# Four cross-attention layers on one core: other orders of work at the layers' edges, and scores with the high and low parts of two heads in one stationary tile

## The chip, the core and the metric

The kernel runs on one NeuronCore of a Trainium2 chip. The metric is the device time of one launch in microseconds (us). The core has TensorE (PE; its weight loads are shown apart as PEld), VectorE (DVE), ScalarE (ACT), GpSimd (POOL), and SyncE (SP), which here issues the DMAs. Each engine runs its own instructions in order and meets the others at semaphores.

## The reference

Four cross-attention layers follow each other on a stream x of 8 batches of 512 tokens by 512 channels. The context has 77 rows of 1024 channels for each batch. Layers 0 and 2 have 16 heads of 64 channels, a bias on four context columns, and an output bias. Layers 1 and 3 normalise x first, and have 16 query heads of 32 channels on 4 key/value heads, so four query heads share the same keys.

```python
# layers 0 and 2
q = x @ Wq; k = ctx @ Wk; v = ctx @ Wv                # 16 heads of 64
logits = einsum('bhqd,bhkd->bhqk', q, k) * 64**-0.5 + col_bias
x = softmax(logits) @ v @ Wo + bo + x
# layers 1 and 3
xn = x * rsqrt(mean(x*x) + 1e-5) * norm_w
q = xn @ wq                                           # 16 heads of 32
k = ctx @ wk; v = ctx @ wv                            # 4 heads of 32
x = softmax(einsum('btgrd,bsgd->bgrts', q, k) * 32**-0.5) @ v @ wo + x
```

## The kernel before

**Numbers in two parts.** Every operand of a large matmul is held as a high part (an fp32r copy, made by ACT) and a low part (the rest, made by DVE or POOL). A product takes three passes into one PSUM bank: high by high, high by low, low by high (`three_passes`, L241 to L243).

**Stages.** A first stage (`context_part`, up to about 267 us) projects the context to keys and values of all layers and writes them to scratch memory. The main part (`whole_block`) runs 130 steps. A unit is one batch, one group of four heads, one layer: 32 units for each layer, kind A for layers 0 and 2 (units 0 to 31 and 64 to 95), kind B for layers 1 and 3 (units 32 to 63 and 96 to 127). In step s every engine works on several units at once: scores and softmax of unit s, queries of unit s+1, transposes of the probabilities of unit s-1 (`turn`, `turned(n)`), the product with the values of unit s-2 (`values`), and the output projection of a batch whose four units are done (`project`).

**Order.** The order is written out by hand for each engine, as a loop over s with one branch for kind A and one for kind B. In a B step TensorE does scores of token tiles 0 and 1, half of the next queries (6 matmuls), scores 2 and 3, a part of the values, `turned(0)`, the other half of the queries, the other values, `turned(1)`, at every fourth step the sums of squares (`stats`), `turned(2)` and the projections. ACT does the exponentials, then the high part of `turned(0)`, of the queries (`split_q`), of the values' product (`split_o`) and of `turned(1)` and `turned(2)`. DVE does for each of four tiles a maximum (L1110) and a subtraction (L1114) that frees the score bank, then a late projection result, the low part of `turned(0)` (L1137), the denominators (L1149, L1152), the low part of the queries (L1121), of the values' product (L1143) and of `turned(1)` (L1137) and `turned(2)` (L1134 in B, L1129 twice in A). There are two score banks, so scores of tile t wait until DVE has done tile t-2 (`s_sub`). In an A step ACT also writes a bias into the score bank ahead of the scores.

**Scores of kind B.** Four heads of 32 channels fill the 128 rows of the stationary tile (the queries). The moving tile is a block-diagonal 128 by 308: the keys of the group four times, 77 columns for each. Three passes of 308 columns make a token tile.

**Projections.** `Plan.projections(s)` says which of a batch's four output chunks are projected in step s: in layers 1 and 3 one chunk a step, at the end of layer 1 two a step; in layers 0 and 2 all four in one step, five steps after the batch began. For the last batch of layers 0 and 2 that is step 33 and step 97, which are B steps. `Plan.late(s)` names the chunk whose result DVE adds in the next step. The weights of a layer come in quarters (`PIECES`), each loaded by SP at the step after the one that consumed the quarter two before.

## Time and profile before

| what | value |
|---|---|
| median of 3 runs | 2091.65 us (2091.45 to 2092.06) |
| the profiled execution's own time | 2090.98 us |
| its span, first to last instruction | 2089.2 us |
| TensorE busy, share of the span | 2044.5 us, 98% |
| VectorE busy | 1390.2 us, 67% |
| ScalarE busy | 966.1 us, 46% |
| GpSimd busy | 644.7 us, 31% |

The table's last four rows are the first part of the profile's page. Busy time of TensorE counts the length of each matmul, and matmuls overlap, so the distance from one start to the next is what a matmul costs; the timeline gives it. The shares are means over stages with different limits.

### The profile page before, as it was taken

To read this page: it belongs to the slowest core of one execution; us is meant where nothing else is said; L and a number is where in the kernel's file an instruction comes from. 1 tells how busy PE (TensorE), PEld (TensorE's weight loads), DVE (VectorE), ACT (ScalarE), POOL (GpSimd) and SP (SyncE) were. 2 spreads that over 40 slices of the span, in tenths; PEclk is the share of its full clock that TensorE was granted. 3 is DMA by queue.
4 is the path that set the end of the run, shared out by engine and by line. 5 is a ranking of instruction groups with operands and counts; after the bars stand their busy time and mean duration, and the time that the engine had idled before them with its cause. 6 is when DMAs were issued, how large, how long until landed. Compare 5 with 4: busy or idle time off the path is not lost.

```text
span 2089.2 us, 31293 instructions
## 1 busy us (share of the span) xinstructions
PE 2044.5 (98%) x11546; PEld 1765.7 (85%) x11546; DVE 1390.2 (67%) x2408; ACT 966.1 (46%) x1814; POOL 644.7 (31%) x519
## 2 busy tenths in 40 slices
PE   8999999999999998999999999999999989999998
PEld 8999988888888886788888888888888867888886
DVE  5332365775568555888888676557755675888885
ACT  3222253553445344655554554335534553555552
POOL 1000042322232254454443341223222443444441
PEclk9999999999999999999999999999999999999999
DMA  7788832222122222343333332212221222333322
GB/s 214 168 171 200 190 91 63 72 67 73 53 72 70 65 75 68 92 108 93 93 90 94 104 96 64 77 53 71 66 73 52 73 85 67 80 91 86 85 72 82
DMA packets 262393, 191.02 MB, mean 91 GB/s; under 512 B 197506, under 2 KB 199970, under 8 KB 259682
## 3 DMA queue, kind: packets, MB, share of 16 engines
q1 hardware_dynamic: 262242, 189.03, 34.6%
q8 instruction: 92, 1.51, 0.3%
q14 instruction: 59, 0.48, 0.1%
HBM read 132.66 MB, written 56.26 MB: 90 GB/s over the span
## 4 chain that ended last, share of the span: by engine, by line
PE 90%; DVE 6%; ACT 1%; DMA 1%; issue 1%; SPq 1%; POOL 0%; DVEq 0%; ACTq 0%
PE acc_bank L846 11%; PE acc_bank L241 8%; PE acc_bank L243 8%; PE acc_bank L242 8%; PE q_bank L804 8%; PE q_bank L808 8%; PE q_bank L806 8%; PE t_bank L826 7%; PE ctx_bank L241 4%; PE ctx_bank L242 4%; PE ctx_bank L243 4%; PE s_bank L767 2%; PE s_bank L241 2%; PE s_bank L764 2%; PE s_bank L770 2%; PE s_bank L243 2%
## 5 line engine op out<-in xcount | busy, mean ns | idle before, releaser
L1262 POOL TENSOR_TENSOR prob<-prob,rinv 128x1232 f32<-128x1232 f32 x128 | 288.5, 2254 | 1044.1 <-DVE rinv L1152 1044.1
L1014 ACT ACTIVATE q_s<-q_bank 128x512 fp32r<-128x512 f32 x192 | 115.1, 599 | 532.9 <-PE q_bank L808 527.0
L846 PE MATMUL acc_bank<-pT_s,vals_s 128*128 128x512 f32 x1024 | 338.1, 415 | 0.0
L1110 DVE TENSOR_REDUCE mx<-s_bank 128x4 f32<-128x308 f32 x512 | 240.5, 470 | 125.7 <-PE s_bank L243 63.5
L804 PE MATMUL q_bank<-x_s,w_s 128*128 128x512 f32 x768 | 319.2, 416 | 4.0 <-POOL w_s L1255 4.0
L808 PE MATMUL q_bank<-x_s,w_s 128*128 128x512 f32 x768 | 313.9, 409 | 0.0
L806 PE MATMUL q_bank<-x_s,w_s 128*128 128x512 f32 x768 | 312.9, 407 | 0.0
L241 PE MATMUL acc_bank<-o_s,w_s 128*128 128x512 f32 x752 | 303.6, 404 | 2.5 <-DVE o_s L1143 2.5
L243 PE MATMUL acc_bank<-o_s,w_s 128*128 128x512 f32 x752 | 296.8, 395 | 0.0
L242 PE MATMUL acc_bank<-o_s,w_s 128*128 128x512 f32 x752 | 296.7, 395 | 0.0
L1005 ACT ACTIVATE prob<-prob,rstd 128x308 f32<-128x308 f32 x256 | 141.2, 555 | 287.3 <-DVE prob L1114 271.5
L1114 DVE TENSOR_TENSOR prob<-s_bank,mx 128x308 f32<-128x308 f32 x512 | 245.2, 479 | 27.4 <-DVE mx L1110 1.4
L1137 DVE TENSOR_TENSOR pT_s<-t_bank,pT_s 128x512 fp32r<-128x512 f32 x256 | 175.8, 687 | 82.3 <-ACT pT_s L1028 82.3
L1166 DVE SCALAR_TENSOR_TENSOR x_back<-acc_bank,bo,x_back 128x512 f32<-128x512 f32 x64 | 47.8, 747 | 259.5 <-PE acc_bank L243 259.5
L846 PEld LDWEIGHTS acc_bank<-pT_s,vals_s 128*128 128x128 f32 x1024 | 190.8, 189 | 28.5
L1028 ACT ACTIVATE pT_s<-t_bank 128x512 fp32r<-128x512 f32 (+1 forms) x320 | 183.3, 590 | 23.8 <-PE t_bank L826 23.6
L826 PE MATMUL t_bank<-ident,prob 128*128 128x128 f32 (+1 forms) x1280 | 184.5, 273 | 1.1 <-DVE pT_s L1137 1.1
L1149 DVE TENSOR_REDUCE sums<-prob 128x16 f32<-128x1232 f32 x128 | 182.5, 1426 | 1.9 <-ACT prob L997 1.9
L826 PEld LDWEIGHTS t_bank<-ident,prob 128*128 128x128 f32 (+1 forms) x1280 | 154.6, 136 | 28.2 <-DVE pT_s L1137 1.6
L241 PEld LDWEIGHTS acc_bank<-o_s,w_s 128*128 128x128 f32 x752 | 141.1, 188 | 34.9 <-DVE o_s L1143 4.1
L243 PEld LDWEIGHTS acc_bank<-o_s,w_s 128*128 128x128 f32 x752 | 141.0, 187 | 34.5
L242 PEld LDWEIGHTS acc_bank<-o_s,w_s 128*128 128x128 f32 x752 | 141.3, 188 | 30.8
(107 smaller groups left out, 4097.2 us busy)
## 6 DMA issues: line engine op xcount, KB each, us to landing
stream<-x_back SPq DMA_DIRECT2D x128, 256.0 KB, 2.6
x_front<-stream SPq DMA_DIRECT2D x96, 256.0 KB, 3.4
x_back<-stream SPq DMA_DIRECT2D x96, 256.0 KB, 4.0
kvw_raw<-kvw SPq DMA_DIRECT2D x17, 1024.0 KB, 8.4
k_scr<-k_out SPq DMA_DIRECT2D x36, 308.0 KB, 9.2
keys_s<-k_scr SPq DMA_DIRECT2D x128, 77.0 KB, 2.4
v_scr<-v_out SPq DMA_DIRECT2D x8, 1024.0 KB
vals_s<-v_scr SPq DMA_DIRECT2D x512, 6.5 KB
```

The source lines that it names most:

```text
L241: pe.matmul(out, weights[0], moving[0], start=start, stop=False)
L242: pe.matmul(out, weights[0], moving[1], start=False, stop=False)
L243: return pe.matmul(out, weights[1], moving[0], start=False, stop=stop)
L804: pe.matmul(out, w[0], x_now[0], start=k == 0, stop=False)
L806: pe.matmul(out, w[0], x_now[1], start=False, stop=False)
L808: mm = pe.matmul(out, w[1], x_now[0], start=False, stop=k == XC - 1)
L826: mm = pe.transpose(t_bank[(3 * u + n) % 2][0:rows, t * P:t * P + P], p, ident[:, :])
L846: mm = pe.matmul(out, w, pT_s[:, part], start=i == mine[0] and part == 2 * n and w is v[0], stop=i == mine[-1] and w is terms[-1][0] and p ...
L1028: act.activation(pT_s[0:rows, 2 * n], t_bank[(3 * u + n) % 2][0:rows, :], ACT.Copy).then_inc(t_hi, 1)
L1110: dve.tensor_reduce(top, scored, AX_X, ALU.max).then_inc(s_max, 1)
L1114: dve.tensor_tensor(prob[:, slot, t].rearrange("q (h n) -> q h n", h=GH), scored, top.unsqueeze(2).broadcast_to([P, GH, CTX]), ALU.subtrac ...
L1262: pool.tensor_tensor(view, view, rinv[:, slot].unsqueeze(2).broadcast_to([P, TILES * GH, CTX]), ALU.mult).then_inc(p_norm, 1)
```

## The change

It has five parts.

1. **Scores of kind B.** A stationary tile now holds 64 rows of high parts of two heads and 64 rows of low parts of the same two heads (`q_s[:, slot, 1, pair]`). The moving tile holds the high part of the keys in its first 154 columns, in every row block. Two matmuls of 154 columns give high by high and low by high for two heads each, and one of 308 columns gives high by low for all four. The keys' DMAs write the same bytes to other columns.
2. **Its operands.** For a B unit ACT makes three copies where it made one (128 rows, then 64 rows twice), and DVE two subtractions of 64 rows where it made one of 128. Each of DVE's two reads 64 rows of the bank and writes the other 64 rows of the tile.
3. **Last batch of layers 0 and 2.** Its four chunks are split between steps 33 and 34 (97 and 98). In step 34 (98), called `ahead`, they come before the values on TensorE, and DVE does the denominators and both results before `turned(0)`.
4. **Steps 0, 1, 31, 63 and 95** (`early`; it acts in the A branch alone). ACT and DVE do the split of the next queries later: the first after the bias of tile 2 (ACT) and after tile 1 (DVE), the second after `turned(1)`. In steps 0 and 1 TensorE spreads the queries over all four tiles.
5. **Weights.** In A steps SP loads the next quarters at the end of the same step instead of at the start of the next.

```diff
@@ Plan
+            projections = [("proj", gb, m) for gb, m in self.projections(s)]
+            if self.ahead(s):
+                acc += projections
             if 0 <= s - 2 < NU:
                 acc += [("pv", s - 2, m) for m in range(kind(s - 2).Q)]
-            acc += [("proj", gb, m) for gb, m in self.projections(s)]
+            if not self.ahead(s):
+                acc += projections
...
-        return found[-1:] if s < NU and kind(s).name == "B" else []
+        return found[-1:] if s < NU and kind(s).name == "B" and not self.ahead(s) else []
+    def ahead(self, s):
+        return 2 * GROUPS <= s < NU and s % (2 * UNITS) == UNITS + 2
+    def early(self, s):
+        return s < 2 or s + 1 < NU and kind(s + 1) is not kind(s)
...
                 elif layer == 1:
                     at += m // 2
+                elif layer % 2 == 0 and b == B - 1:
+                    at += m // 2
@@ sync
-                    keys = keys_s[:, slot].bitcast(F32).rearrange("q (h n) -> q h n", h=2)
                     for r in range(GH):
-                        sp.dma_start(keys[32 * r:32 * r + 32, :, CTX * r:CTX * r + CTX],
+                        keys = keys_s[32 * r:32 * r + 32, slot, 0:2 * CTX * (2 + r - r % 2)].bitcast(F32)
+                        sp.dma_start(keys.rearrange("q (h a n) -> q h a n", h=2, n=CTX)[:, :, r % 2],
                                      k1_scr[p, b, 32 * g:32 * g + 32]).then_inc(keys_loaded[slot], 16)
...
-                for n in plan.pieces(s - 1):
-                    if n + 2 < len(PIECES):
-                        load_weights(n + 2)
+                if s and kind(s - 1).name == "B":
+                    for n in plan.pieces(s - 1):
+                        if n + 2 < len(PIECES):
+                            load_weights(n + 2)
...
                     load_vals(s)
+                if s < NU and kind(s).name == "A":
+                    for n in plan.pieces(s):
+                        if n + 2 < len(PIECES):
+                            load_weights(n + 2)
@@ tensor
-                    keys = keys_s[:, slot].rearrange("q (h n) -> q h n", h=2)
-                    three_passes(pe, out[:, 0:SC], [q_s[:, slot, h, 0, tok] for h in range(2)],
-                                 [keys[:, h] for h in range(2)], True, True).then_inc(s_mm, 1)
+                    for pair in range(2):
+                        pe.matmul(out[:, PAIR * pair:PAIR * (pair + 1)], q_s[:, slot, 1, pair, tok],
+                                  keys_s[:, slot, 0:PAIR], start=pair == 0, stop=False, skip_group_check=True)
+                    pe.matmul(out[:, 0:SC], q_s[:, slot, 0, 0, tok], keys_s[:, slot, PAIR:PAIR + SC], start=False,
+                              stop=True, skip_group_check=True).then_inc(s_mm, 1)
...
-                if a:
+                if a and s < 2:
+                    for t in range(TILES):
+                        beside(scores(s, t), q, 6)
+                        if t >= 2:
+                            turned(t - 2)
+                    turned(2)
+                elif a:
...
                     run(scores(s, 3), 1)
+                    if plan.ahead(s):
+                        for gb, m in plan.projections(s):
+                            project(gb, m)
                     run(v, 3)
@@ scalar
-                    act.activation(q_s[:, u % 2, 0, m], q_bank[item % 2][:, :], ACT.Copy).then_inc(q_hi, 1)
+                    high = act.activation(q_s[:, u % 2, 0, m], q_bank[item % 2][:, :], ACT.Copy)
+                    if kind(u).name == "B":
+                        for pair in range(2):
+                            rows = slice(64 * pair, 64 * pair + 64)
+                            high = act.activation(q_s[rows, u % 2, 1, pair], q_bank[item % 2][rows, :], ACT.Copy)
+                    high.then_inc(q_hi, 1)
...
-                    next(q, None)
+                    if not plan.early(s):
+                        next(q, None)
                     bias(s, 2)
...
                     bias(s + 1, 1)
+                    next(q, None)
                     exps(s, 1)
@@ vector
+                        for pair in range(2):
+                            rows, other = slice(64 * pair, 64 * pair + 64), slice(64 - 64 * pair, 128 - 64 * pair)
+                            low = dve.tensor_tensor(q_s[other, u % 2, 1, pair], q_bank[item % 2][rows, :],
+                                                    q_s[rows, u % 2, 0, m].bitcast(F32), ALU.subtract)
...
-                    next(q, None)
+                    if not plan.early(s):
+                        next(q, None)
                     tile_scores(s, 1)
...
                         rest_o(s - 2, pv - 1)
+                    next(q, None)
                     denominators(s)
...
+                    if plan.ahead(s):
+                        denominators(s)
+                        for gb, m in plan.projections(s):
+                            add_result(gb, m)
                     turned(0)
-                    if s < NU:
+                    if s < NU and not plan.ahead(s):
                         denominators(s)
```

## Rows read from the trace of the kernel before

**Rows 1.** The page: busy us (share of the span) and instructions of each engine.
```profile
PE 2044.5 (98%) x11546; PEld 1765.7 (85%) x11546; DVE 1390.2 (67%) x2408; ACT 966.1 (46%) x1814; POOL 644.7 (31%) x519
```
**Rows 2.** Table by stretch, steps 109 to 112: length, busy us (x), granted clock, DMA.
```profile
1861.10:1903.90 42.80, 42.80 (x233) 36.50 (x232) 35.77 (x66) 23.63 (x45) 18.62 (x12) 1.00 0.34 90
```
**Rows 3.** Waits in the same stretch: who waited for whom, us in total, times, longest.
```profile
DVE mx L1110 <- PE s_bank L243: 3.9, 8, 1.3
```
**Rows 4.** Timeline of PE, an A step: start, length, engine, line, out<-in.
```profile
500.18 0.23 PE L764 MATMUL s_bank<-keys_s,q_s 128*128 128x154 f32 x1
...
500.98 0.24 PE L764 MATMUL s_bank<-keys_s,q_s 128*128 128x154 f32 x1
```
**Rows 5.** Timeline of PE, two B steps of the steady part.
```profile
1871.62 0.30 PE L241 MATMUL s_bank<-keys_s,q_s 128*128 128x308 f32 x1
1871.76 0.30 PE L242 MATMUL s_bank<-keys_s,q_s 128*128 128x308 f32 x1
...
1872.46 0.39 PE L804 MATMUL q_bank<-x_s,w_s 128*128 128x512 f32 x1
1872.69 0.39 PE L806 MATMUL q_bank<-x_s,w_s 128*128 128x512 f32 x1
...
1874.26 0.41 PE L241 MATMUL s_bank<-keys_s,q_s 128*128 128x308 f32 x1
1874.50 0.30 PE L242 MATMUL s_bank<-keys_s,q_s 128*128 128x308 f32 x1
...
1882.15 0.30 PE L241 MATMUL s_bank<-keys_s,q_s 128*128 128x308 f32 x1
...
1893.49 0.30 PE L241 MATMUL s_bank<-keys_s,q_s 128*128 128x308 f32 x1
```
**Rows 6.** Timeline of DVE, the same part.
```profile
1873.72 0.48 DVE L1114 TENSOR_TENSOR prob<-s_bank,mx 128x308 f32<-128x308 f32 x1
...
1882.77 0.48 DVE L1110 TENSOR_REDUCE mx<-s_bank 128x4 f32<-128x308 f32 x1 [0.55 <-PE s_bank L243]
```
**Rows 7.** Timeline of DVE, step 36 (no projection).
```profile
858.75 0.48 DVE L1110 TENSOR_REDUCE mx<-s_bank 128x4 f32<-128x308 f32 x1
...
865.68 0.25 DVE L1152 RECIPROCAL rinv<-sums 128x16 f32<-128x16 f32 x1
865.85 0.63 DVE L1121 TENSOR_TENSOR q_s<-q_bank,q_s 128x512 fp32r<-128x512 f32 x1
866.40 0.68 DVE L1143 TENSOR_TENSOR o_s<-acc_bank,o_s 128x512 fp32r<-128x512 f32 x1
866.99 0.68 DVE L1137 TENSOR_TENSOR pT_s<-t_bank,pT_s 128x512 fp32r<-128x512 f32 x1
867.70 0.69 DVE L1134 TENSOR_TENSOR pT_s<-t_bank,pT_s 64x512 fp32r<-64x512 f32 x1
868.42 0.48 DVE L1110 TENSOR_REDUCE mx<-s_bank 128x4 f32<-128x308 f32 x1
```
**Rows 8.** Timeline of DVE and ACT, step 32: ops on part of the rows.
```profile
804.13 1.20 ACT L1023 ACTIVATE pT_s<-t_bank 64x512 fp32r<-64x512 f32 x2
...
805.93 1.38 DVE L1129 TENSOR_TENSOR pT_s<-t_bank,pT_s 32x512 fp32r<-32x512 f32 x2
```
**Rows 9.** Timeline of PE, steps 31, 32 and 33, with idle before and releaser.
```profile
785.98 0.34 PE L764 MATMUL s_bank<-keys_s,q_s 128*128 128x154 f32 x1 [1.01 <-ACT s_bank L990]
...
796.58 0.42 PE L241 MATMUL s_bank<-keys_s,q_s 128*128 128x308 f32 x1 [2.60 <-DVE prob L1114]
...
815.87 0.50 PE L241 MATMUL acc_bank<-o_s,w_s 128*128 128x512 f32 x1 [1.25 <-DVE o_s L1143]
```
**Rows 10.** Table by stretch, steps 0 and 1: columns as in rows 2.
```profile
267.34:289.24 21.90, 20.13 (x109) 16.91 (x108) 12.61 (x24) 10.80 (x22) 8.96 (x8) 0.92 0.22 65
```
**Rows 11.** Timeline of PE, step 1: its first matmul, and one in the slow stretch.
```profile
277.18 0.34 PE L764 MATMUL s_bank<-keys_s,q_s 128*128 128x154 f32 x1 [0.83 <-ACT s_bank L990]
...
278.33 0.63 PE L804 MATMUL q_bank<-x_s,w_s 128*128 128x512 f32 x1
```

More of the change, by code:

```diff
@@ L948, in _ @@
                     turned(2)
-                    for gb, m in plan.projections(s):
-                        project(gb, m)
+                    if not plan.ahead(s):
+                        for gb, m in plan.projections(s):
+                            project(gb, m)
                 elif s == NU:
@@ L1120, in rest_q @@
                     dve.wait_ge(q_hi, plan.q_splits[("q", u, m)] + 1)
-                    dve.tensor_tensor(q_s[:, u % 2, 1, m], q_bank[item % 2][:, :], q_s[:, u % 2, 0, m].bitcast(F32),
-                                      ALU.subtract).then_inc(q_out, 1)
+                    if kind(u).name == "A":
+                        low = dve.tensor_tensor(q_s[:, u % 2, 1, m], q_bank[item % 2][:, :],
+                                                q_s[:, u % 2, 0, m].bitcast(F32), ALU.subtract)
+                    else:
+                        for pair in range(2):
+                            rows, other = slice(64 * pair, 64 * pair + 64), slice(64 - 64 * pair, 128 - 64 * pair)
+                            low = dve.tensor_tensor(q_s[other, u % 2, 1, pair], q_bank[item % 2][rows, :],
+                                                    q_s[rows, u % 2, 0, m].bitcast(F32), ALU.subtract)
+                    low.then_inc(q_out, 1)
                     yield
@@ L1212, in _ @@
                         add_result(gb, m)
+                    if plan.ahead(s):
+                        denominators(s)
+                        for gb, m in plan.projections(s):
+                            add_result(gb, m)
                     turned(0)
-                    if s < NU:
+                    if s < NU and not plan.ahead(s):
                         denominators(s)
@@ L1224, in _ @@
                     for gb, m in plan.projections(s):
-                        if (gb, m) not in plan.late(s):
+                        if (gb, m) not in plan.late(s) and not plan.ahead(s):
                             add_result(gb, m)
```

## The prediction

> **What bounds the kernel now.** The page comes first: TensorE is busy 98% of the span, DVE 67% [rows 1]. So TensorE looks like the only bound, and a change that takes columns from it like a sure gain. The table by stretch says otherwise for the B layers: in 42.80 us, four steps, DVE is busy 35.77, 84% [rows 2]. The waits of that stretch show what is left: DVE waits for scores 3.9 us in 8 waits, two a step [rows 3]. The timelines of the two engines show how close they run. A B step without `stats` takes 10.53 us on TensorE (1871.62 to 1882.15), one with it 11.34 (1882.15 to 1893.49) [rows 5]; DVE starts a unit after 0.55 idle [rows 6]. The reader is to see that TensorE is the bound by about half a microsecond a step, and not everywhere: in step 36, which has no projection, DVE goes from one unit to the next without a wait (867.70 to 868.42), so its own loop, 858.75 to 868.42, is the step: 9.67 us [rows 7].
>
> **Scores, on TensorE.** Distances between starts are prices. A 512-column matmul costs 0.23 (1872.46 to 1872.69), one of 308 columns 0.14 [rows 5]. From one L764 to the next in an A step lie three matmuls of 154 columns and two of 512: 0.80 less 0.46 leaves 0.113 for each of 154 [rows 4]. So a token tile goes from 3 x 0.14 to 2 x 0.113 + 0.14: 0.06 less. A unit saves 0.24, and 64 units 15 us. That is all the change can take from TensorE's work.
>
> **Its operands, on DVE.** One subtraction of the queries becomes two. Their cost depends on overlap. Between ops that begin at row 0 the next starts before the last has ended: reciprocal to queries 0.17, queries to values' product 0.55, that to `turned(1)` 0.59. But to L1134, which reads rows 0 to 63 and writes rows 64 to 127, it takes 0.71 after an op of 0.68, and away from it 0.72 after 0.69 [rows 7]; two L1129 in a row take 1.38, no overlap [rows 8]. The new subtractions move rows exactly as L1134 does, so I price them by it: reciprocal to the first 0.28 (0.25 + 0.03), first to second 0.70, second to L1143 0.72, in all 1.70 where 0.17 + 0.55 = 0.72 stood: +0.98 a B unit. The other end is one more op at the overlapped 0.55.
>
> The Trainium skill, VectorE: DVE Perf Modes, section "Two Vector instructions with no wait between them", has a rule for this: an instruction with an input or output that starts in another group of 32 rows than the last instruction's first input, or output, in the same memory waits until all earlier ones have finished. It agrees with the 0.71 and 0.72 here. It holds the second subtraction and L1143 behind it too, which no row here shows in that form. By the rule a unit pays 0.98, without it 0.55.
>
> ACT gets two more copies. Two copies of 64 rows end 1.20 after the first starts [rows 8], so the high part is ready some 1.1 later. ACT is busy 23.63 of 42.80 [rows 2]; in the steady step it splits the queries while DVE still reduces the denominators, so I cost this at nothing there, and at 0.1 where a step is entered late.
>
> **A steady B step.** DVE's loop becomes 9.67 + 0.98 = 10.65. (A projection's result, 0.68, fits into DVE's wait for ACT's first transposed copy.) TensorE by itself would need 10.53 - 0.24 = 10.29 or a little more, because scores of tile 3 already wait for DVE's tile 1: DVE ends it at 1873.72 + 0.48, TensorE starts at 1874.26, and the second matmul follows after 0.24, not 0.14 [rows 5, 6]. So DVE becomes the bound: 10.65, +0.12 a step. A `stats` step gives TensorE 0.81 more and stays its own: 11.34 - 0.12 = 11.22. After it DVE starts early, and its wait for tile 2's scores, about a quarter of a microsecond, is back: 10.88. Steps 38 to 62 hold 6 of 11.22, 6 of 10.88 and 13 of 10.65: 271.1 us, against 19 x 10.53 + 6 x 11.34 = 268.1. That is +3.0 a layer, +6.0 for layers 1 and 3. The whole saving on TensorE is used up, and more.
>
> **Entry into the B layers (steps 31 to 37).** `early` lifts the wait of 1.01 for the bias. But the next stop is scores of tile 2 in step 32, released by DVE after 2.60 idle [rows 9]. DVE's row of work up to there is not shortened; it gets one query op more, most of it in its own idle time: +0.15. In steps 32 and 33 DVE sets the start of the next scores, and of the first projection (1.25 idle behind L1143 [rows 9]): +1.0 each. Splitting the four chunks moves 11.2 us (48 x 0.23) of projection from step 33 to 34. There the early denominators (0.25 + 1.46 or so) leave DVE's row behind the projections, but the second half of the queries still comes after them: three copies and two subtractions, 1.7 + 1.4 us, against the 2.0 of values and transposes that TensorE has left. So it waits; I work out +0.35 for the step. Steps 35 and 36 are DVE's loop: +0.98 each. Step 37: 10.65 for 10.52, +0.13. Sum 4.6 a layer, 9.2 for two. Steps 63 and 127 have no B queries behind them and keep part of the saving: -0.8 together.
>
> **Steps 0 and 1** take 21.90 [rows 10]. Their 48 query matmuls at 0.23, 48 of scores at 0.113 and 12 transposes at 0.11 come to 17.8: 4.1 are lost, to waits (0.83 for a bias the longest) and to a stretch in which a 512 lasts 0.63 instead of 0.39: the clock was granted at 1.2 GHz, not 2.4, behind these waits [rows 11]. The new order has the bias in time. But the second query split now stands, on ACT, behind a bias that needs DVE's last tile, and the next step's scores need the split: 1.8 us by the same durations in step 1, 0.4 in step 2. That idle lies in otherwise dense matmuls, so I expect full clock: a gain of 4.1 - 2.2 = 1.9; between 0 and 4.1.
>
> **Weights.** SP loads the quarters for step 30 one step sooner, but what step 31 waits for is POOL's low part, which stands behind a memset that waits for step 30's scores. Nothing gained. SP's new wait comes after its value loads, with only stores behind it that are due later still.
>
> **Sum.** 6.0 + 9.2 - 0.8 - 1.9 = +12.5 us on the profiled execution's own 2090.98 (its span 2089.2 and 1.8 around it): 2103.5. The median of the runs is 0.7 above that execution: 2104.
>
> **Rivals.**
> - *The new subtractions overlap.* A unit pays 0.55, DVE's loop is 10.22 and TensorE keeps the steady steps at about 10.44: -0.09 x 50 = -4.5. Entry 2.1 a layer, +4.2. With -0.8 and -1.9 the sum is -3.0: 2088.7. For it: DVE's 3.9 us of waits [rows 3]. Against: L1134 and L1129 [rows 7, 8]. 9%.
> - *Faster, TensorE alone counts.* If DVE's waits take the new op everywhere, the time is 2091.65 - 15 - 2 = 2074.6. Its place is the wait of scores 3 for tile 1, its price 0.24 a unit; it decides if DVE's second wait shrinks as the first does. Against it: step 36, where both were gone and 9.67 was the step. 4%.
> - *Slower still, the clock.* TensorE gets up to 3 us idle a step in steps 32 to 37 and 96 to 101, on fewer columns; behind such waits the clock fell in step 1 [rows 11]. Six more such stretches, each worth some 1.7 us if nothing hides it (about seven 512s, each 0.24 longer), give 2114. In steps that DVE bounds most is hidden. 7%.
> - *It does not do what it says.* If a matmul of 154 columns cost 0.14 in this place, TensorE would save nothing. DVE is the bound anyway: 2104 to 2106, inside the forecast.
>
> **Chances.** Forecast 80%, rivals 9, 4 and 7%. About 0.2%, 4.2 us, is what a measurement of this kernel can tell from no change. Faster by more: the second rival, and the first with a good start: 7%. Within: the rest of the first, and a forecast off by 8 us: 10%. Slower: 83%. The forecast's own terms run from 0 to -4.1 (start), 3 to 6 a layer (entry) and 1.5 to 4 a layer (steady): 2097 to 2110. To leave out no more than 2 in 10 I give 2093 to 2112.
>
> **What would show it.** DVE's timeline: L1121, L1121, L1143 start 0.70 and 0.72 apart, and L1110 starts without idle in steps without `stats`; 0.55 apart is the first rival. TensorE's: the two matmuls of 154 columns 0.11 apart, steps of 10.65 with idle released by DVE L1114 where rows 5 show none, steps 35 and 36 at 10.65, and in step 1 no wait for the bias but one for L1121. The forecast is wrong if steady steps last 10.5 or less, or if steps 31 to 37 together are not 4 to 5 us longer.

## The result, and the profile after

The changed kernel takes 2114.81 us (median of 4 runs, 2113.61 to 2116.17), the kernel before in the same session 2091.86 (2091.45 to 2092.09): ratio 1.0112, 95% interval 1.0098 to 1.0125. Slower, as forecast, but by 23.0 us where 12.4 were forecast, and outside the range of 2093 to 2112. The profiled execution took 2116.17 against 2090.98, 25.2 us more; the accounts below are of these two. One of the five executions of e1 below took 3981.76 us, in a slow state, and is left out of its median.

The first part of the page, against [rows 1]:

```profile
PE 2051.7 (97%) x11546; PEld 1753.9 (83%) x11546; DVE 1446.8 (68%) x2472; ACT 1035.0 (49%) x1942; POOL 645.1 (31%) x519
```

The shares barely moved, since they are means over all stages. DVE has 64 more operations, ACT 128. The table by stretch, steps 109 to 112, against [rows 2], and the waits of the same stretch, against [rows 3]:

```profile
1881.27:1925.18 43.91, 43.28 (x234) 35.53 (x233) 39.47 (x70) 28.05 (x53) 18.82 (x13) 1.00 0.35 90
```
```profile
DVE pT_s L1182 <- ACT pT_s L1064: 2.0, 4, 0.5
PEld s_bank L800 <- DVE prob L1152: 1.7, 4, 0.5
DVE mx L1148 <- PE s_bank L802: 0.9, 3, 0.5
```

The two stretches were cut by hand; from first scores to first scores the four steps last 43.84 instead of 42.90. DVE works 39.5 us of them instead of 35.8, and its waits for scores fell from 3.9 to 0.9 us. The granted clock is 1.00. DVE is the bound there, though not quite alone: 0.9 us are left. DVE's timeline in step 112, against [rows 7]:

```profile
1922.53 0.25 DVE L1197 RECIPROCAL rinv<-sums 128x16 f32<-128x16 f32 x1
1922.81 1.39 DVE L1165 TENSOR_TENSOR q_s<-q_bank,q_s 64x512 fp32r<-64x512 f32 x2
1924.23 0.69 DVE L1188 TENSOR_TENSOR o_s<-acc_bank,o_s 128x512 fp32r<-128x512 f32 x1
1924.84 0.68 DVE L1182 TENSOR_TENSOR pT_s<-t_bank,pT_s 128x512 fp32r<-128x512 f32 x1
```

From reciprocal to L1188 are 1.70 us, where 0.72 stood: exactly the +0.98 of the forecast. TensorE's timeline, against [rows 5]: the scores of one tile, and the first scores of steps 113, 115 and 116.

```profile
1914.77 0.34 PE L800 MATMUL s_bank<-keys_s,q_s 128*128 128x154 f32 x2
1914.95 0.34 PE L802 MATMUL s_bank<-keys_s,q_s 128*128 128x308 f32 x1
1915.13 0.35 PE L800 MATMUL s_bank<-keys_s,q_s 128*128 128x154 f32 x2
...
1925.18 0.35 PE L800 MATMUL s_bank<-keys_s,q_s 128*128 128x154 f32 x2
...
1946.87 0.35 PE L800 MATMUL s_bank<-keys_s,q_s 128*128 128x154 f32 x2
...
1958.60 0.34 PE L800 MATMUL s_bank<-keys_s,q_s 128*128 128x154 f32 x2
```

A tile costs 0.36 (1914.77 to 1915.13), the 0.37 of the forecast. Where the profiled 25.2 us lie, in lengths between the first scores of steps in TensorE's two timelines:

| steps | forecast | measured |
|---|---|---|
| 0 to 2 | -1.9 | -1.4 (33.31 to 31.86) |
| 31 to 37 | +4.6 | +6.2 (101.50 to 107.71) |
| 95 to 101 | +4.6 | +9.0 (100.08 to 109.06) |
| 38 to 62 | +3.0 | +4.4 (269.02 to 273.40) |
| 102 to 126 | +3.0 | +5.5 (267.99 to 273.49) |
| 63 and 127 | -0.8 | +0.3 |
| all else (the first stage +1.0) | 0 | +1.3 |

### The profile page after: what moved, and what is told of

It reads as the page before. It is cut to its first block, busy times and chain, and to the rows that moved or that the text cites. A ratio compares the mean times of both kernels' runs of the same rounds, so it can differ in the third digit from the quotient of the medians.

```text
span 2114.4 us, 31485 instructions
## 1 busy us (share of the span) xinstructions
PE 2051.7 (97%) x11546; PEld 1753.9 (83%) x11546; DVE 1446.8 (68%) x2472; ACT 1035.0 (49%) x1942; POOL 645.1 (31%) x519
## 4 chain that ended last, share of the span: by engine, by line
PE 72%; DVE 21%; ACT 3%; issue 2%; DMA 1%; SPq 1%; POOL 0%; DVEq 0%; ACTq 0%
PE acc_bank L867 8%; PE q_bank L825 7%; PE q_bank L827 7%; PE q_bank L829 7%; PE acc_bank L255 7%; PE acc_bank L256 7%; PE acc_bank L257 7%; PE t_bank L847 5%; DVE prob L1152 4%; DVE mx L1148 3%; DVE q_s L1165 3%; PE ctx_bank L255 3%; PE ctx_bank L256 3%; PE ctx_bank L257 3%; DVE sums L1194 3%; DVE pT_s L1182 3%
## 5 line engine op out<-in xcount | busy, mean ns | idle before, releaser
L1182 DVE TENSOR_TENSOR pT_s<-t_bank,pT_s 128x512 fp32r<-128x512 f32 x256 | 175.8, 687 | 84.5 <-ACT pT_s L1064 84.5
L1064 ACT ACTIVATE pT_s<-t_bank 128x512 fp32r<-128x512 f32 (+1 forms) x320 | 183.2, 589 | 38.9 <-PE t_bank L847 38.1
L255 PEld LDWEIGHTS acc_bank<-o_s,w_s 128*128 128x128 f32 x752 | 141.5, 188 | 42.9 <-DVE o_s L1188 12.9
```

What stands on the lines that cost most here:

```text
L255: pe.matmul(out, weights[0], moving[0], start=start, stop=False)
```

## The experiments

All were timed in 5 rounds beside the kernel before on the same chip. "Diff" is to its median there (2090.2 to 2091.2; for the changed kernel 2091.86, as above). The sessions ran on different chips, and the difference of two diffs is uncertain by some 4 us, as the intervals show; step lengths repeat much better. The next two columns are the lengths of steps 31 to 37 and 95 to 101, the last is steps 109 to 112, four steady ones, all from TensorE's timeline of the profiled execution.

| kernel | median | diff | ratio, 95% | 31 to 37 | 95 to 101 | four |
|---|---|---|---|---|---|---|
| before | | | | 101.5 | 100.1 | 42.90 |
| changed | 2114.8 | +23.0 | 1.0098 to 1.0125 | 107.7 | 109.1 | 43.84 |
| e1 packing alone | 2121.7 | +31.3 | 1.0138 to 1.0166 | 109.6 | 110.9 | 43.82 |
| e2 orders alone | 2085.4 | -5.0 | 0.9966 to 0.9985 | 99.5 | 97.7 | 42.96 |
| e3 one subtraction | 2084.2 | -6.2 | 0.9961 to 0.9984 | 100.9 | 100.5 | 42.39 |
| e4 and one copy | 2078.1 | -12.3 | 0.9929 to 0.9954 | 98.9 | 97.6 | 42.46 |
| e5 two wide ones | 2095.1 | +4.6 | 1.0013 to 1.0031 | 103.7 | 105.7 | 42.73 |
| e6 in place | 2109.9 | +19.4 | 1.0073 to 1.0101 | 105.7 | 105.8 | 43.45 |
| e7 o first | 2132.2 | +41.7 | 1.0184 to 1.0212 | 111.4 | 111.3 | 44.63 |
| e8 GpSimd | 2097.5 | +7.0 | 1.0017 to 1.0040 | 106.6 | 106.1 | 42.44 |
| e9 hybrid | 2078.3 | -12.9 | 0.9930 to 0.9955 | 99.5 | 99.2 | 42.45 |
| e10 early splits | 2089.3 | -1.9 | 0.9982 to 0.9999 | 100.0 | 99.0 | 42.95 |
| e11 ahead | 2089.0 | -2.2 | 0.9985 to 1.0002 | 99.0 | 100.6 | 42.90 |
| e12 two subtractions | 2113.1 | +22.0 | 1.0094 to 1.0125 | 105.7 | 103.4 | 44.22 |
| e13 one copy | 2108.5 | +18.3 | 1.0070 to 1.0097 | 103.6 | 105.2 | 43.85 |
| e14 short stats | 2106.7 | +16.5 | 1.0065 to 1.0090 | 107.5 | 106.1 | 43.17 |

**e1, e2: the two halves of the change.** e1 is the changed kernel with parts 3 to 5 undone; e2 has them alone:

```diff
e1  def ahead(self, s), def early(self, s):
+        return False
     projections, the A branch for s < 2 and the weights as before
...
e2  scores, load_keys, split_q, rest_q as before
```

> The changed kernel with its order edits (parts 3 to 5) undone: only the packed scores and their operands (parts 1 and 2) stay. Theory: the loss is the packing's, by VectorE's two subtractions that do not overlap (+0.98 us a B unit, 64 units): steady steps of layers 1 and 3 as in the changed kernel, 43.85 us for four where 42.90 stood (+10 in all), the entries +0.98 for each of steps 31 to 36 or so (+10 to +12), steps 0 and 1 as before: +20 to +23 on the kernel before, 2112 to 2115. Rival, the orders at the edges cost it: their undoing leaves only the steady part, +6 to +10, 2098 to 2102.

> The kernel before with the order edits alone (parts 3 to 5); scores, query operands and keys as before. Theory: steps 0 and 1 give back 1.5 us, the split of the last batch's projections and the later query splits move little: -1 to -4, 2088 to 2091. Rival, the orders cost the time: steps 31 to 37 and 95 to 101 longer by 3 to 5 us a layer, 2096 to 2102.

The loss is the packing's, the orders gain 5.0 us alone. With the packing they gain 8.3: by so much is e1 slower than the changed kernel, counted by the differences. So there were two changes of opposite sign. Both runs left their ranges: e1 took 2121.7 where 2112 to 2115 was expected, its entries being 18.9 us longer than before and not 10 to 12, and e2 gained more than the 1 to 4 us expected. The table of steps 0 and 1 in it, and in the changed kernel, against [rows 10]:

```profile
268.02:288.35 20.33, 18.56 (x110) 15.69 (x108) 12.36 (x24) 10.86 (x22) 8.99 (x8) 1.00 0.22 59
```
```profile
268.35:288.44 20.09, 18.21 (x109) 15.55 (x108) 12.26 (x23) 11.05 (x22) 9.99 (x9) 1.00 0.23 62
```

With the old order, still behind the bias waits, but at clock 1.00, the two steps take 20.33; the 21.90 of [rows 10] had 0.92. The new order's 0.24 is lost again in step 2 (11.77 for 11.42). So the 1.4 us "gained" at the start are the one stretch at the lower clock (1.2 of 2.4 GHz), which the old order met in two profiled executions (before, e10) and not in two others (e1, e11). None of the 12 profiled executions with the new order met it in step 1; whether the new order prevents it is not shown.

**e3, e4: without the price of the operands.**

```diff
e3  rest_q
-                    else: for pair in range(2): ... 64 rows each
+                    dve.tensor_tensor(q_s[:, u % 2, 1, m], q_bank[item % 2][:, :], q_s[:, u % 2, 0, m].bitcast(F32), ...)
e4  split_q, besides
-                    if kind(u).name == "B": for pair in range(2): ... 64 rows each
```

> The changed kernel with one change: for a B unit VectorE makes one subtraction of 128 rows where it made two of 64 (the low part of heads 2 and 3 is left out of its tile, and a low part stands where the high one of heads 2 and 3 should; TensorE and ScalarE do what they do in the changed kernel). Theory: VectorE pays 0.98 us a B unit less, its loop is 9.67 to 9.77 again, TensorE is the bound of the steady steps and keeps its 0.24 a unit less a small wait for tile 1: four steady steps in 42.0 to 42.3 where the changed kernel has 43.85 (-20 to -23 in all), the entries -10 or so: 2080 to 2086. Rival, the clock or the extra copies of ScalarE are what costs: 2100 or more.

> As the run before, and ScalarE's two extra copies of 64 rows left out as well (the tile of heads 0 and 1 then holds low parts alone, that of heads 2 and 3 old values). Theory: ScalarE's copies are hidden in steady steps and cost at most 0.1 to 0.5 us in the steps at the entry: 0 to 4 us under the run before it. Rival, ScalarE's 1.2 us a unit lies in the loop (VectorE's low parts wait for its copies): 8 us or more under it.

e3's time lies in its range, its four steps just above theirs (42.39 for 42.0 to 42.3). With one subtraction the changed kernel is 29.2 us faster, more than the whole loss of 23.0: without VectorE's second operation the change would gain. TensorE then keeps 0.5 us in four steps, not the 0.96 of its columns. e4 missed: 6.1 us under e3, not 0 to 4. The steady steps are equal, so ScalarE's copies cost nothing there; the difference is at the entries (steps 33 and 34 together: 43.9 us in e3, 41.7 in e4).

**e12, e13: the same two prices beside VectorE's.** e12 is e2 with the changed kernel's `rest_q`; e13 is the changed kernel with ScalarE's one copy.

> The order edits with VectorE's two subtractions of the changed kernel and nothing else of the packing: TensorE makes three passes of 308 columns as before, ScalarE one copy (the low tile is half filled, so scores of kind B lack part of their low part). VectorE's price with nothing in return. Theory: once VectorE sets the steps, TensorE's saving is worth only what lies on the stretch that TensorE still sets (tile 3 of a stats step to the next step's first scores), some 0.1 us in four steps: 43.9 to 44.1 for four steady steps, the entries 2 us a layer shorter than the changed kernel's for want of ScalarE's copies: 2109 to 2113. Rival, TensorE's 0.24 a unit counts in every unit: 44.8 for four, 2118 to 2122.

> The changed kernel with ScalarE's two extra copies of 64 rows left out (the high halves of the paired tiles hold old numbers); VectorE's two subtractions and TensorE's packed matmuls stay. Theory: the prediction's entry was too small because ScalarE's 1.2 us were costed at nothing: without them the entries fall by 2 us or more a layer (to 105.0 to 106.0 us for steps 31 to 37, and 103 to 106 for 95 to 101), steady steps stay at 43.85 for four, the whole 2106 to 2110. Rival, the clock or VectorE alone makes the excess at the entry: entries as in the changed kernel, 2113 to 2116.

They close a ladder by the differences: orders -5.0 (e2), VectorE's subtractions +27.0 (e12 less e2), TensorE's packed matmuls -3.7 (e13 less e12), ScalarE's copies +4.6 (changed less e13): together +23.0. At 4 us of uncertainty a rung, the last two rest on the step lengths: e13's steps 38 to 62 and 102 to 126 are 2.3 us shorter than e12's in each layer, and the copies show in single steps below. At the entries (31 to 37 and 95 to 101 together, profiled executions) the same ladder reads -4.4, +11.9, -0.3 and +8.0, together +15.2. VectorE's 27.0 are 0.42 a unit, of 0.98: the rest fell into its waits. TensorE's saving of 15 us of columns gave 3.7, and would give 7.3 without VectorE's price (e4 less e2). e12's 44.22 for four lies above the theory's 43.9 to 44.1 and below the rival's 44.8: 0.37 of TensorE's 0.96 counts although VectorE is the bound. e13 shows where ScalarE's copies sit. In step 34 of the changed kernel, the chain of waits (start, length, what), then DVE's and PE's timelines; and DVE's in step 34 of e13:

```profile
847.30 0.60 ACT q_s L1045
847.90 0.48 ACT q_s L1049
...
848.38 0.60 ACT q_s L1049
...
849.01 0.69 DVE q_s L1165
...
849.71 0.69 DVE q_s L1165
```
```profile
849.01 1.39 DVE L1165 TENSOR_TENSOR q_s<-q_bank,q_s 64x512 fp32r<-64x512 f32 x2 [1.78 <-ACT q_s L1049]
...
850.50 0.42 PE L800 MATMUL s_bank<-keys_s,q_s 128*128 128x154 f32 x2 [1.21 <-issue]
```
```profile
844.55 1.39 DVE L1160 TENSOR_TENSOR q_s<-q_bank,q_s 64x512 fp32r<-64x512 f32 x2 [0.71 <-ACT q_s L1045]
```

VectorE waits 1.07 longer for the copies. TensorE enters step 35 after 1.21 us idle; the row names no engine, but the chain does: the second L1165 ends at 850.40, the scores start at 850.50. In e13 no idle is marked there, and the step is 19.08 instead of 20.16. The same wait stands in the steps before it, here DVE in step 31 of the changed kernel and then of e13:

```profile
786.29 1.39 DVE L1165 TENSOR_TENSOR q_s<-q_bank,q_s 64x512 fp32r<-64x512 f32 x2 [1.00 <-ACT q_s L1049]
```
```profile
784.99 1.39 DVE L1160 TENSOR_TENSOR q_s<-q_bank,q_s 64x512 fp32r<-64x512 f32 x2
```

Step by step, changed less e13: in the six entry steps whose granted clock is the same to 0.01 in both, 31, 32, 34, 95, 97 and 98, the copies cost 0.96, 0.95, 1.08, 0.96, 0.00 and 1.09, together 5.0 us. The other 3.0 of the 8.0 lie in step 33 (25.22 for 24.09, clock 0.93 for 1.00) and step 96 (14.83 for 12.99, clock 0.65 for 0.87), where copies and clock are not told apart. In the steady steps the same copies end while VectorE still reduces the denominators.

**e5, e6: is it the operation, or that it does not overlap?**

```diff
e5  rest_q, for kind B
     (in place of the two of 64 rows)
+    dve.tensor_tensor(q_s[:, u % 2, 1, 1], q_bank[...][:, :], q_s[:, u % 2, 0, m].bitcast(F32), ALU.subtract)
+    dve.tensor_tensor(q_s[:, u % 2, 1, 0], q_bank[...][:, :], q_s[:, u % 2, 0, m].bitcast(F32), ALU.subtract)
...
e6  split_q: high part of either pair to rows 64:128; rest_q: pair 1 first, low part of either pair to rows 0:64
-    q_s[other, u % 2, 1, pair]
+    q_s[0:64, u % 2, 1, pair]
```

> The changed kernel with VectorE's two subtractions of 64 rows that move rows replaced by two of 128 rows in place, into the two tiles (they overwrite high parts, so the scores of kind B are of other numbers; the count of operations stays). It tells the price of the second operation from the price of not overlapping. Theory: the two begin at row 0 as their neighbours do and overlap; distances reciprocal to first 0.17, first to second 0.55, second to values' product 0.55, 1.27 where the changed kernel has 1.70; VectorE's loop is 10.3 and TensorE is the bound of most steps: four steady steps in 42.5 to 43.0, the whole 2088 to 2096. Rival, the number of operations is what costs and not their rows: distances stay 0.70, 43.8 for four steps, 2112 to 2116.

> The changed kernel with other row halves: low parts of either pair stand in rows 0 to 63 and high parts in rows 64 to 127 of their tile, so VectorE moves rows only for heads 2 and 3 (first) and works in place for heads 0 and 1 (second, right before the values' product), and ScalarE moves rows for heads 0 and 1. The result is the reference's. Theory: the second subtraction and the values' product both begin at row 0 everywhere, so only that distance falls, from 0.72 to 0.55; reciprocal to first 0.28 and first to second 0.70 stay. 0.17 less a unit in steps that VectorE sets: 43.2 to 43.6 for four steady steps, the whole 5 to 11 us under the changed kernel, 2103 to 2109. Rival, subtractions of 64 rows never overlap whatever their rows: no distance changes, 2113 to 2116.

DVE's timelines, e5 and then e6:

```profile
1883.95 0.25 DVE L1193 RECIPROCAL rinv<-sums 128x16 f32<-128x16 f32 x1
1884.12 0.63 DVE L1160 TENSOR_TENSOR q_s<-q_bank,q_s 128x512 fp32r<-128x512 f32 x1
1884.66 0.68 DVE L1162 TENSOR_TENSOR q_s<-q_bank,q_s 128x512 fp32r<-128x512 f32 x1
1885.26 0.68 DVE L1184 TENSOR_TENSOR o_s<-acc_bank,o_s 128x512 fp32r<-128x512 f32 x1
```
```profile
1890.71 0.25 DVE L1198 RECIPROCAL rinv<-sums 128x16 f32<-128x16 f32 x1
1891.00 1.39 DVE L1166 TENSOR_TENSOR q_s<-q_bank,q_s 64x512 fp32r<-64x512 f32 x2
1892.31 0.67 DVE L1189 TENSOR_TENSOR o_s<-acc_bank,o_s 128x512 fp32r<-128x512 f32 x1
```

Two operations that both begin at row 0 cost 1.31 from reciprocal to L1184, the two that move rows 1.70. The count of operations is the same, so the 0.39 between them is missing overlap, and it makes 18.3 us of the 23.0 (changed less e5). The second operation itself, overlapped, costs 10.8 (e5 less e3). In e6 the two start 0.70 apart and L1189 begins 0.61 behind the second, which works in place, so 1.60: the saving is 0.10 and not 0.17, and the four steady steps fall by 4 x 0.10. e6's whole gain on the changed kernel is 3.6 us by the differences, not 5 to 11. That L1189 overlaps a subtraction of 64 rows excludes the rival that the number of rows prevents it. The Trainium skill, VectorE: DVE Perf Modes, section "Two Vector instructions with no wait between them", would have exactly this: the in-place subtraction is held (it waits for all earlier ones to end), because its input starts in another quadrant, a group of 32 rows, than the last one's, and L1189 is not. The trace agrees with 0.70 and 0.61.

**e7, e14: why four steady steps take 43.84 and not 43.4.** In every fourth step TensorE waits in the projection for VectorE's low part of the last values' product. e7 puts that first:

```diff
+                    if pv == 1:
+                        rest_o(s - 2, 0)
                     next(q, None)
                     next(q, None)
...
e14 stats
-                for t in range(TILES):
-                    mm = pe.matmul(out[:, t:t + 1], x_power[:, t * P:t * P + P], mean_w[:, :], ...)
+                mm = pe.matmul(out[:, 0:TILES], x_power[:, 0:P], x_power[:, 0:TILES], start=True, stop=True)
```

> The changed kernel with one order changed on VectorE: in B steps the low part of the values' product comes before the low parts of the queries. It tells whether TensorE's wait for that low part in the projection of every fourth step (0.23 us, behind which the step lasts 11.28) costs anything. Theory: no, VectorE is then busy and would start the next step no sooner; the step's excess is VectorE's loop catching up. Steady steps 43.8 to 44.0 for four, the whole within 2 us of the changed kernel, up to 4 us more if the queries' low parts now come too late for the next scores. Rival, the wait is what costs: 0.5 to 0.9 less for four steady steps, 6 to 11 us in all, 2104 to 2109.

> The changed kernel with the sums of squares cut from eight small matmuls to one product of four columns (0.8 us of TensorE in every fourth B step becomes some 0.2; the norm's factor is then another number). Theory: the steady cycle of four steps is longer than VectorE's own loop (4 x 10.75) because TensorE enters the stats step behind VectorE and cannot make up its 0.8 us, so VectorE waits for the next step's scores: without it four steps take 43.0 to 43.3 instead of 43.85, the whole 7 to 10 us less, 2104 to 2108. Rival, the excess is the late start of the projection in every fourth step: 43.6 to 43.9, 2111 to 2115.

e7 cost 18.7 us more, against both texts. DVE's timeline in it:

```profile
1913.08 0.25 DVE L1197 RECIPROCAL rinv<-sums 128x16 f32<-128x16 f32 x1
1913.70 0.69 DVE L1188 TENSOR_TENSOR o_s<-acc_bank,o_s 128x512 fp32r<-128x512 f32 x1 [0.37 <-ACT o_s L1069]
1914.43 1.39 DVE L1165 TENSOR_TENSOR q_s<-q_bank,q_s 64x512 fp32r<-64x512 f32 x2
```

The product's high part is not ready, since ScalarE makes it after the queries' copies: 0.37 of wait in three of four steps and 0.11 in the fourth. And L1182 now follows a subtraction of the queries, where it starts 0.73 after it; behind L1188 it was 0.61. From the reciprocal to L1182 that makes 2.77 for 2.31, and 0.79 us in four steady steps. e14's four steps came out as its theory had them, 43.17; the whole fell by 6.4 us, just short of the 7 to 10. The cycle in the changed kernel, PE and DVE in steps 115 and 116:

```profile
1949.96 0.45 PE L800 MATMUL s_bank<-keys_s,q_s 128*128 128x154 f32 x2 [0.27 <-DVE prob L1152]
```
```profile
1947.94 0.48 DVE L1148 TENSOR_REDUCE mx<-s_bank 128x4 f32<-128x308 f32 x1
...
1959.16 0.48 DVE L1148 TENSOR_REDUCE mx<-s_bank 128x4 f32<-128x308 f32 x1 [0.50 <-PE s_bank L802]
```

VectorE sets three steps of the cycle, together 32.1 us (10.41, 11.28, 10.41). In the fourth, TensorE can start tile 3's scores only when VectorE has done tile 1 (1949.96), and then has 8.64 us of its own, `stats` included, to the scores of step 116 (1958.60); VectorE waits for those 0.50, and 0.17 for tile 2's behind them. The bound changes hands within a cycle, and each engine starts its part late.

**e8, e9: packed scores without VectorE.** e8: from the third unit of a B layer on, ScalarE writes one more full copy of the queries, and GpSimd makes both low parts from it. e9: the same from the eighth unit on, the first seven as in the kernel before.

```diff
+    def pooled(self, u):
+        return kind(u).name == "B" and u % UNITS >= 7      # e8: 2
...
+            def rest_q(u):                                  # GpSimd, ahead of normalise(u - 1); its waits left out
+                for pair in range(2):
+                    rows = slice(64 * pair, 64 * pair + 64)
+                    low = pool.tensor_tensor(q_s[rows, u % 2, 1, pair], q_f[rows, :], q_s[rows, u % 2, 0, 0].bitcast(F32), ALU.subtract)
```

> A version meant to keep the packed scores without their price on VectorE: from the third unit of each B layer on, ScalarE writes a full copy of the queries besides the high parts (one more copy of 128 rows) and GpSimd computes both low parts from it, in place by rows, with ScalarE moving the rows of the high parts. The result is the reference's. Theory: VectorE's loop falls to about 9.1 to 9.8, TensorE is the bound with 10.4, 11.2 in a stats step, 42.4 for four steady steps: 2080 to 2088, under the kernel before and about level with the order edits alone. Rival, the bound goes to another engine: GpSimd's two operations (1.27 each) and ScalarE's third extra copy make the queries late for the next scores or the probabilities late for the transposes, steps of 10.8 or more, 2105 or more.

> A version put together from the runs so far, with the reference's result: the order edits of the changed kernel; the first 7 units of each B layer as in the kernel before (three passes, one copy, one subtraction), the other 25 packed, with GpSimd making the low parts as in the run of GpSimd's queries. At the switch GpSimd clears the key tiles once more. Theory: the entries are those of the order edits alone (99.5 and 97.7 us for steps 31 to 37 and 95 to 101), the steady steps those of GpSimd's queries (42.45 for four, 265.6 for steps 38 to 62): 5 to 6 us under the order edits alone, 2078 to 2081, 10 to 12 under the kernel before. Rival: the switch costs what it gives (the clearing or GpSimd's and ScalarE's longer rows make step 38 or 39 late by some us, or the clock falls there): 2083 to 2088.

e8's steady steps were as expected (42.44), its entries were not (212.7 us for the two together, e2 197.2), and its 2097.5 missed the 2080 to 2088. GpSimd and TensorE in its step 35:

```profile
857.05 1.26 POOL L1341 TENSOR_TENSOR q_s<-rest,q_s 64x512 fp32r<-64x512 f32 x1 [3.67 <-ACT rest L1059]
859.00 1.27 POOL L1341 TENSOR_TENSOR q_s<-rest,q_s 64x512 fp32r<-64x512 f32 x1 [0.68 <-ACT q_s L1063]
```
```profile
860.37 0.42 PE L808 MATMUL s_bank<-keys_s,q_s 128*128 128x154 f32 x2 [1.68 <-issue]
```

Without a projection behind the queries nothing hides the longer row: ScalarE's four copies and GpSimd's two operations, the last of which ends at 860.27. e9 leaves the entries' packing out and packs only from unit 7 of a layer on. Its table for four steady steps:

```profile
1863.19:1905.67 42.48, 42.48 (x234) 35.62 (x233) 33.96 (x62) 30.62 (x57) 28.98 (x21) 1.00 0.37 88
```

TensorE 42.48 of 42.48, VectorE 34.0 where the changed kernel has 39.5. e9 is the fastest kernel here that leaves nothing out, 2078.3, ratio 0.9943 (0.9930 to 0.9955), as expected (2078 to 2081), and 36 us under the changed one.

**e10, e11: the order edits one by one.** On the kernel before, e10 has `early` for steps 31, 63 and 95 alone, e11 has `ahead` with the chunks split over two steps.

> The kernel before with one part of the order edits alone: the later query splits of ScalarE and VectorE in steps 31, 63 and 95 (not in 0 and 1). Theory: most of what the order edits give at the entries is from here, as the bias no longer stands behind the split: steps 31 and 32, 95 and 96 together 2 to 3.5 us shorter, the whole 2087 to 2089. Rival, the gain is the split of the projections: no change here, 2090 to 2091.

> The kernel before with another part of the order edits alone: the last batch's four chunks of projection in layers 0 and 2 split over steps 33 and 34 (97 and 98), the second two ahead of the values. Theory: steps 33 and 34 together 0.4 to 1.2 us shorter a layer, the whole 2088.5 to 2090. Rival, it is the larger part of the gain of the order edits: 2086 to 2088.

-1.9 and -2.2 us by medians (ratios 0.9990 and 0.9994, and e11's interval holds 1): too little for the medians to say which carries more. The step lengths show both. In e10 the wait for the bias is gone and steps 31 and 95 are 1.37 and 1.05 us shorter, each at the same granted clock as before (0.88 and 0.87, 1.00 and 1.00). In e11 steps 33 and 34 together are 1.17 shorter (97 and 98: 1.16) and step 35 is 0.23 longer (99: 0.25), all at clock 1.00. So either part is worth some 2 us. What spoils the totals is the clock. The same code, step 95, in e2 and in e9:

```profile
1682.87:1694.91 12.04, 9.97 (x67) 8.64 (x66) 10.42 (x19) 7.94 (x16) 7.09 (x7) 1.00 0.40 115
```
```profile
1679.02:1692.32 13.30, 11.32 (x68) 9.96 (x66) 10.44 (x19) 7.92 (x16) 7.09 (x7) 0.87 0.44 126
```

## Why the prediction was right and wrong

- **Direction and mechanism: right.** VectorE's two subtractions do not overlap, cost +0.98 a unit and make VectorE the bound (the 1.70 above; e3, e5). TensorE's saving per tile was right to 0.01. Steps 35 and 36 were forecast at 10.65 and took 10.67 and 10.75. The forecast was 10.6 us too low by medians and 12.7 in the profiled execution: 6.0 of it at the entries, 3.9 in the steady steps, 2.8 elsewhere.
- **Entry into the B layers: the step that failed.** +9.2 was forecast, +15.2 measured in the profile. The words were "I cost this at nothing there, and at 0.1 where a step is entered late", of ScalarE's two copies. They cost 4.6 us by medians (changed less e13), and 8.0 in the profiled entries (216.8 against 208.8), 5.0 of them at equal clock; without them the entries are +2.1 and +5.1 on before, 7.2 in all, under the forecast's 9.2. I had named the place (step 34, "three copies and two subtractions") and counted TensorE's cover of 2.0 against it, but gave the same 1.1 us no price in steps 31, 32 and 33. There VectorE waits 1.00, 0.30 and 0.63 us for the copies, and not at all in e13.
- **Two more terms of the entry.** The subtractions cost 11.9 us there (e12 less e2). The order edits, whose effect on steps 31 and 32 was put at nothing ("DVE's row of work up to there is not shortened"), take 2.0 and 2.4 us out of the two profiled entries (e2), and that hid part of the miss. In step 31 the copies' +0.96, the subtractions' +0.60 (e12 less e2) and the order's gain of 1.37 (e2, e10) nearly cancel: +0.20 was measured and +0.15 forecast, by luck. And step 37 took 11.74 us in the kernel before, not the 10.52 of the forecast, and 12.16 in the changed one: +0.42 for +0.13.
- **The clock: in part.** The rival of a lower clock gave 2114 and 7%, and the time is 2114.8. That the numbers meet is mostly luck: the steady steps' 3.9 us arose at clock 1.00, and 5.0 us of the copies at equal clock. The clock did play a part. The profiled entries ran at a mean of 0.95 and 0.92 where those of before ran at 0.97 and 0.98, and one step with such a stretch takes 1.26 more (12.04 to 13.30). It accounts for the difference between the two layers' entries (+6.2 and +9.0) with the same code: step 31 ran at 0.88 before and 0.89 after and is 0.20 longer (14.88), step 95 at 1.00 before and 0.89 after and is 1.75 longer (14.87). How much of the +15.2 is the clock in all was not separated.
- **A steady B step: size off.** Forecast 43.4 for four, measured 43.84, +3.9 us over both layers. "TensorE keeps the `stats` step, VectorE the others" took the larger of two loops step by step. The three other steps came out as forecast in sum, 32.1 for 32.2, though unevenly: 10.41 in two of them and 11.28 in the third. The miss is the stats step: it begins late by what VectorE lagged before it, and took 11.75, not 11.22 (e14).
- **Steps 0 and 1: size right, reason half right.** -1.9 forecast, -1.4 measured over steps 0 to 2. The forecast counted on full clock and on shorter waits; the first gave all of it (e1). The waits did change places as forecast (none for the bias, 1.50 us for L1160 in step 1), with no gain.
- **Weights: right.** TensorE's wait for GpSimd's low part of the weights in step 31 is 1.98 us before and after.
- **Steps 63 and 127:** -0.8 forecast, +0.3 measured; in 127 the chain to the last output gained nothing. **The first stage** lost 1.0 us in the profiled execution; e1 to e14, with the same code there, start their steps at 267.5 to 268.6 (before 267.3, changed 268.4), so it is no part of the change.
- **Sums.** 48 x 0.23 is 11.0, not 11.2. The forecast's own terms, added up, run from 2096 to 2111 and not from 2097 to 2110. Neither moves the forecast or its range.

## What to carry to other kernels

A second operation is priced by the distance between starts, and that depends on where its rows begin: keep an engine's consecutive operations on the same starting rows, or give the odd ones to an engine with slack. An engine with half its time idle, as ScalarE here, still has no slack in the steps where its result is awaited; ask for each stage what covers the addition, above all at the edges. When two engines are within a few per cent of each other, follow a whole cycle of waits: here the maximum of two loops, step by step, was too small by 1% (43.4 for 43.84). Time the parts of a mixed change apart: here one was worth -5 and the other +28. Compare single steps at equal granted clock where medians are too coarse.

## What the hardware showed

- In step 34 of the changed kernel ScalarE's first copy of 64 rows starts 0.50 behind the one of 128 rows, the second, which begins at row 64, 0.59 behind that, and the next one of 128 rows 0.62 behind the second; two of 128 rows start 0.48 to 0.49 apart (L1069 to L1064). Half the rows do not cost less. The dearer ones are those behind a change of the starting row; no run tests that as the cause.
- GpSimd's subtraction takes 1.27 us for 64 rows (e8), about what it takes for 128 (L1288, 2.55 for two).
- A matmul of 154 columns costs 0.11 also in pairs on full tiles (0.36 a tile less 0.14 for the 308), far from half of that 0.14: fewer columns save little here.
